# Chained graph layers on one core: orders of their own for the first and last seven turns, VectorE's constants placed later, no filler matmuls

## The chip, the cores and the metric

One core of a Trainium2 chip runs the whole program. The metric is the device time of one execution in microseconds (us); lower is better. TensorE (PE) does the matmuls, VectorE (DVE), ScalarE (ACT) and GpSimd (POOL) the elementwise work, SyncE's queue (SP) starts most of the DMAs. Each engine runs its own list of instructions in order, and they meet only at semaphores.

## What is computed

`x` is (128, 128, 256) and `adj` (128, 128, 128): 128 graphs of 128 nodes. Four layers follow one another, each with its own weights:

```python
def reference(x, adj, ...):
    x = _L0_gnn_ref(x, adj, ...)   # 8-head attention, + log(clip(adj)), out projection, layer norm
    x = _L1_gnn_ref(x, adj, ...)   # one-head attention, logits = q + k^T, mask, leaky relu, softmax
    x = _L2_gnn_ref(x, adj, ...)   # 8-head attention, + a + c^T + log(adj + eps)
    x = _L3_gnn_ref(x, adj, ...)   # like layer 1, other weights
    return x
# layer 0
q = (x @ Wq.T + bq).reshape(b, n, H, DK).transpose(0, 2, 1, 3)      # k, v likewise
logits = jnp.einsum('bhqd,bhkd->bhqk', q, k) / np.sqrt(DK)
logits = logits + jnp.log(jnp.clip(adj, ADJ_MIN, None))[:, None, :, :]
attn = jax.nn.softmax(logits, axis=-1)
out = jnp.einsum('bhqk,bhkd->bhqd', attn, v)
out = out.transpose(0, 2, 1, 3).reshape(b, n, d) @ Wo.T + bo
return _layer_norm(x + out, gamma, beta)
# layer 1
logits = q + jnp.swapaxes(k, 2, 1)
masked = logits + (1.0 - adj_mat) * NEG_INF
masked = jnp.where(masked >= 0, masked, LEAKY_SLOPE * masked)
out = jnp.einsum('bnm,bmh->bnh', jax.nn.softmax(masked, axis=-1), feat_proj)
return out + feats
```

## The kernel before

Two graphs make a group, so there are 64 groups (0 to 63), and every group passes through the four layers. The work of one group is cut into named steps. A step is a name, a layer or stream, and a part; a text that says "`q` of layer 2, group 63" means all instructions of that step. Stream A is the attention of layer 0, stream B that of layer 2.

The steps of an attention layer are, in the order in which they depend on one another:

- `turn_x`: ACT rounds the layer's transposed input to a high part (`xt_hi`), POOL (layer 0) or DVE (the others) makes the low part (`xt_lo`). In layer 1 PE first transposes the input.
- `v`, `k`, `q`: PE multiplies by the weights in three passes of high and low parts (lines 911 to 913, 12 matmuls of 256 columns a step; layer 2's `v` is two parts of 6), ACT moves the result to SBUF.
- `scores`: PE, L976, and in stream B also L985. `max`: DVE takes the least of each row from the four score banks (L800). `max_parts`: two small DVE steps in stream B. `turn_max`: PE turns those (L1079), ACT copies. `again`: the scores turned (L976). `shift`: the maxima are subtracted (L999).
- `soft`: ACT takes the exponentials (L563, L567). `weigh`: DVE multiplies three of four banks by the adjacency (L824), POOL the first (L486).
- `den`: PE sums (L1020), DVE takes the reciprocal and splits it (L831 to L835), POOL spreads it to `inv_parts` (L492). `use`: PE multiplies the weights by `v` (L1011), ACT copies the result. `wide`: PE spreads the reciprocals (L1025), DVE multiplies (L841).
- Layer 0 then has `split` (ACT and DVE halve the result into `ot_hi`, `ot_lo`), `out_proj` in two parts (PE, DVE adds and takes statistics), `rstd` (POOL, L498 and L502) and `norm` (DVE L877, ACT L573). Layer 2 has `sum` (DVE, L848).

Layers 1 and 3 have `fc` in two parts (12 matmuls in all), `mask` (PE L1113, DVE L759), `leak` (ACT, DVE), `exp`, `inv` (ACT, DVE), `turn_p` (PE L1119, ACT copies to `fpt`) and `mix` (PE L1125, DVE adds). `adj_t` and `penalty` prepare the adjacency. SP loads four arrays for each group, each load behind the last reader of the same buffer of the group before.

The table ORDER gives every engine one fixed list of steps for a turn, each step with a lag. Turn t does, in that list's order, step (lag, name) of group t minus lag. So a steady turn holds every step once, of up to seven different groups. In the first and the last turns the steps of groups that do not exist are left out, and what remains keeps its order:

```python
    def steps(self, engine):
        for lag, name, where, n in ORDER[engine]:
            if self.holds(self.t, lag):
```

Eight PSUM banks are shared out by position in TensorE's list. Before a step fills a bank, PE waits until the last reader of the bank's former contents is done (`wait_drained`).

Setup is woven into group 0. DVE first makes small constants (`pick`, `own`, `spread`, `minus_pick`, `low_row`; L684 to L696), then the low parts of the weights (`low_parts(FIRST)`: q0, k0, v0; `low_parts(SECOND)`: five more). Eight steps of groups 0 and 1 on PE are preceded by filler matmuls (L1063), whose result is overwritten:

```python
FILLERS = {(("den", "A", 0), 0): 6, (("out_proj", "0", 0), 0): 12, (("turn_max", "A", 0), 1): 10,
           (("den", "A", 0), 1): 4, (("mix", "1", 0), 0): 5, (("out_proj", "0", 0), 1): 4,
           (("turn_max", "A", 0), 2): 7, (("mix", "1", 0), 1): 5}
```

## Time and profile before

| | |
|---|---|
| median of 3 runs | 1814.74 us (1814.38 to 1816.23) |
| the profiled execution | 1811.3 us, of which the span is 1809.5 us |
| PE busy | 1750.8 us, 97% of the span |
| DVE, ACT, POOL busy | 1474.9, 1371.8, 731.3 us |
| filler matmuls | 53 records, 8.95 us busy |

The span runs from the first to the last instruction. An engine's busy time is the union of its instructions. Matmul ends are modelled, so the distance from start to start is the better measure of a row of matmuls. "Idle before" in a row is the time in which the engine did nothing ahead of that instruction, and the name behind the arrow is what ended it.

### The profile page before, as it was taken

The page shows a single profiled execution, that of the slowest core. Times are in us where ns is not written, and L with a number is a line of the kernel's source. Part 1 is how long each engine was busy: PE and PEld are TensorE (multiplying, and loading weights), DVE is VectorE, ACT ScalarE, POOL GpSimd, SP SyncE. Part 2 cuts the span into 40 slices and gives each one's busy share as a digit, 9 for nine tenths or more (in the row PEclk, how much of TensorE's full clock was granted, in tenths as well). Part 3 has the DMA queues.
Part 4 walks back from the last instruction along what each step waited for, and adds up shares of the span by engine and source line. Part 5 has one row for each costly group of instructions (what it writes and reads, how often), then busy time and mean ns, then how long its engine had stood idle before and what let it go on. Part 6 is the DMA issues. An engine that isn't in the chain of part 4 may idle for free.

```text
span 1809.5 us, 68658 instructions
## 1 busy us (share of the span) xinstructions
PE 1750.8 (97%) x28065; PEld 1642.0 (91%) x28065; DVE 1474.9 (82%) x3361; ACT 1371.8 (76%) x3792; POOL 731.3 (40%) x797
## 2 busy tenths in 40 slices
PE   6899999999999999999999999999999999999985
PEld 6799999999999999999999999999999999999974
DVE  4678888888888888888888888888888888888873
ACT  3577787787787787787877778778778777778773
POOL 3344443443444344344344344444444344344321
PEclk8999999999999999999999999999999999999997
DMA  3011111011011011011011011111111101101100
GB/s 108 28 37 37 37 49 48 26 49 49 26 49 49 26 49 48 26 49 49 27 47 49 30 44 49 38 37 49 34 40 49 49 26 49 47 28 49 35 13 18
DMA packets 48260, 74.55 MB, mean 41 GB/s; under 512 B 5456, under 2 KB 21968, under 8 KB 47952
## 3 DMA queue, kind: packets, MB, share of 16 engines
q1 hardware_dynamic: 47376, 69.49, 12.0%
q8 instruction: 227, 3.72, 0.9%
q10 hardware_dynamic: 576, 0.68, 0.2%
q14 instruction: 81, 0.66, 0.1%
HBM read 53.37 MB, written 16.78 MB: 39 GB/s over the span
## 4 chain that ended last, share of the span: by engine, by line
PE 88%; ACT 3%; DMA 2%; DVE 2%; issue 2%; POOL 2%; SPq 0%; POOLq 0%; DVEq 0%; ACTq 0%
PE banks L911 16%; PE banks L976 14%; PE banks L913 14%; PE banks L912 14%; PE banks L1125 7%; PE banks L1020 6%; PE banks L1011 6%; PE banks L999 3%; DMA x_t<-x_t_dram 2%; PE banks L1025 2%; PE banks L1085 2%; PE banks L1119 2%; PE banks L1113 2%; POOL weights_B L486 1%; PE banks L985 1%
## 5 line engine op out<-in xcount | busy, mean ns | idle before, releaser
L486 POOL TENSOR_TENSOR weights_B<-weights_B,adj 128x512 f32<-128x512 f32 x64 | 115.2, 1801 | 297.4 <-ACT weights_B L567 297.4
L492 POOL TENSOR_TENSOR inv_parts_A<-inv_both_A,own 128x512 fp32r<-128x512 f32 x64 | 66.6, 1041 | 305.0 <-DVE inv_both_A L835 305.0
L800 DVE TENSOR_REDUCE least_cols_A<-banks 128x4 f32<-128x512 f32 x256 | 159.0, 684 | 32.4 <-PE banks L976 32.3
L800 DVE TENSOR_REDUCE least_B<-banks 128x4 f32<-128x512 f32 x256 | 173.2, 681 | 13.6 <-PE banks L985 13.6
L911 PE MATMUL banks<-w_hi_v,xt_hi 128*128 128x258 f32 (+1 forms) x512 | 157.4, 308 | 13.2 <-DVE w_lo_v L677 11.5
L911 PE MATMUL banks<-w_hi_f,xt_hi 128*128 128x258 f32 x512 | 163.5, 319 | 3.0 <-DVE xt_lo L677 1.5
L641 ACT ACTIVATE fp<-banks 128x258 f32<-128x258 f32 x256 | 92.1, 390 | 93.8 <-PE banks L913 93.8
L567 ACT ACTIVATE banks<-banks,v_B 128x256 f32<-128x256 f32 x384 | 153.7, 475 | 0.0
L911 PE MATMUL banks<-xt_hi,w_hi_k 128*128 128x256 f32 x512 | 151.7, 296 | 0.0
L913 PE MATMUL banks<-w_lo_f,xt_hi 128*128 128x258 f32 x512 | 146.3, 286 | 0.0
L1125 PE MATMUL banks<-fpt,fp 128*128 128x128 f32 x1024 | 143.5, 283 | 2.8 <-ACT fpt L662 2.7
L913 PE MATMUL banks<-w_lo_v,xt_hi 128*128 128x258 f32 (+1 forms) x512 | 145.2, 284 | 0.0
L912 PE MATMUL banks<-w_hi_v,xt_lo 128*128 128x258 f32 (+1 forms) x512 | 145.0, 283 | 0.0
L912 PE MATMUL banks<-xt_hi,w_lo_k 128*128 128x256 f32 x512 | 144.9, 283 | 0.0
L912 PE MATMUL banks<-w_hi_f,xt_lo 128*128 128x258 f32 x512 | 144.7, 283 | 0.0
L1125 PEld LDWEIGHTS banks<-fpt,fp 128*128 128x128 f32 x1024 | 130.0, 193 | 16.0 <-issue 15.4
L913 PE MATMUL banks<-xt_lo,w_hi_k 128*128 128x256 f32 x512 | 144.4, 282 | 0.0
L913 PE MATMUL banks<-xt_lo,w_hi_q 128*128 128x256 f32 x512 | 144.0, 281 | 0.0
L912 PE MATMUL banks<-xt_hi,w_lo_q 128*128 128x256 f32 x512 | 143.6, 280 | 0.0
L911 PE MATMUL banks<-xt_hi,w_hi_q 128*128 128x256 f32 x512 | 143.5, 280 | 0.0
L831 DVE RECIPROCAL banks<-banks 128x128 f32<-128x128 f32 x128 | 122.5, 957 | 9.7 <-PE banks L1020 9.7
L458 POOL TENSOR_TENSOR xb_t<-sum_t,out_col 128x512 f32<-128x512 f32 x64 | 66.5, 1039 | 156.2 <-DVE sum_t L848 156.2
(192 smaller groups left out, 6210.4 us busy)
## 6 DMA issues: line engine op xcount, KB each, us to landing
x_t<-x_t_dram SPq DMA_DIRECT2D x64, 256.0 KB, 3.6
x_in<-x_dram SPq DMA_DIRECT2D x64, 256.0 KB, 3.6
out_dram<-x_out SPq DMA_DIRECT2D x64, 256.0 KB, 2.4
adj_t<-adj_t_dram SPq DMA_DIRECT2D x64, 128.0 KB, 3.4
adj<-adj_dram SPq DMA_DIRECT2D x64, 128.0 KB, 2.0
scratch<-weights_dram SPq DMA_DIRECT2D x9, 256.0 KB, 6.9
scratch<-weights_dram ACTq DMA_DIRECT2D x2, 256.0 KB, 4.6
out_bias<-L_gnn_bo_dram ACTq DMA_DIRECT2D x1, 128.0 KB, 6.9
```

The costliest lines, as they stand in the source:

```text
L486: pool.tensor_tensor(units, units, weight_of[where][:, G.four, :, :].unsqueeze(2).broadcast_to([P, GROUP, 2, P]), ALU.mult).then_inc(first ...
L567: last = act.activation(to[:, cols(g, 2 * P)], x[:, cols(g, 2 * P)], ACT.Exp, bias=v["B"][:, G.odd, g, DIM + 1:WIDE], scale=-1.0)
L641: act.activation(fp[where][:, n, :], bank[b][:, 0:WIDE], ACT.Copy).then_inc(fp_ready[where], 1)
L800: dve.tensor_reduce(to, bank[SCORE_BANKS[n]].rearrange("p (u m) -> p u m", u=UNITS), axis=AX.X, op=ALU.min).then_inc(maxed[where], 1)
L831: dve.reciprocal(bank[b][:, 0:P], bank[b][:, 0:P]).then_inc(inverted[where], 1)
L911: pe.matmul(out_ap, left_hi(k), right_hi(k), start=(k == 0), stop=False)
L912: pe.matmul(out_ap, left_lo(k), right_hi(k), start=False, stop=False)
L913: last = pe.matmul(out_ap, left_hi(k), right_lo(k), start=False, stop=(k == KT - 1))
L976: last = pe.matmul(bank[SCORE_BANKS[r]][:, cols(u)], left[row_group(r), G.odd, half, cols(g)], right[row_group(r), G.odd, half, cols(g)], ...
L1011: last = pe.matmul(to[row_group(r), cols(u)], v[s][:, G.odd, g, head:head + HEAD_DIM], weights[s][:, r, cols(u)], start=True, stop=True)
L1020: last = pe.matmul(to[row_group(r), 0:P], sums[:, u, :], weights[s][:, r, cols(u)], start=(u == 0), stop=(u == UNITS - 1), skip_group_chec ...
L1125: last = pe.matmul(to[:, cols(k * GROUP + g)], fp[layer][:, g, cols(k)], fpt[layer][:, g, :], start=True, stop=True)
```

## The change

Three things are changed.

1. Two new tables, EARLY and LATE, give the order of tensor, vector, scalar and gpsimd for their first and last steps (159, 180, 163 and 46 early ones, 86, 86, 110 and 24 late ones). They hold the same steps as before. Between them ORDER applies as it stands. SP's order is not touched. The semaphore counts of the banks are now counted from the resulting list.
2. DVE makes its constants behind `low_parts(FIRST)`.
3. FILLERS is empty.

```diff
+EARLY = {
+    "tensor": [
+        (0, "v", "0", 0), (0, "k", "0", 0), (0, "q", "0", 0), (0, "scores", "A", 0), (0, "turn_max", "A", 0),
...
+LATE = {
+    "tensor": [
+        (-1, "k", "0", 0), (-2, "out_proj", "0", 0), (-1, "q", "0", 0), (-2, "out_proj", "0", 1), (-3, "k", "2", 0),
...
-FILLERS = {(("den", "A", 0), 0): 6, (("out_proj", "0", 0), 0): 12, (("turn_max", "A", 0), 1): 10,
-           (("den", "A", 0), 1): 4, (("mix", "1", 0), 0): 5, (("out_proj", "0", 0), 1): 4,
-           (("turn_max", "A", 0), 2): 7, (("mix", "1", 0), 1): 5}
+FILLERS = {}
...
+def all_steps(engine, groups):
+
+    order = [(t - lag, name, where, n) for t in range(FIRST_LAG, groups + LAST_LAG + 1)
+             for lag, name, where, n in ORDER[engine] if 0 <= t - lag < groups]
+    early = list(EARLY.get(engine, ()))
+    late = [(groups + back, name, where, n) for back, name, where, n in LATE.get(engine, ())]
+    assert sorted(early) == sorted(order[:len(early)]) and sorted(late) == sorted(order[len(order) - len(late):])
+    return early + order[len(early):len(order) - len(late)] + late
...
-            dve.wait_ge(const_ready, CONSTANTS)
-            dve.tensor_reduce(pick[:, :], pick_all[:, :, :], axis=AX.X, op=ALU.add).then_inc(setup_dve, 1)
...
+            def constants():
+                dve.wait_ge(const_ready, CONSTANTS)
+                dve.tensor_reduce(pick[:, :], pick_all[:, :, :], axis=AX.X, op=ALU.add).then_inc(setup_dve, 1)
...
                 if (name, where, n) == ("max", "A", 0):
                     low_parts(FIRST)
+                    constants()
                     low_parts(SECOND)
```

Below, the line numbers of the changed kernel are some 190 higher, since the two tables stand above: its L877 is L684 of the kernel before, its L1105 is L911.

VectorE at the very start, before (the constants are L684 to L696, the low parts L677):

```order
3 L684 TENSOR_REDUCE pick<-pick_all 128x4
4 L685 TENSOR_REDUCE own<-own_all 128x4
5 L688 TENSOR_REDUCE weights_B<-weights_B 128x128
6 L691 CAST spread<-weights_B 128x128
7 L693 TENSOR_TENSOR minus_pick<-pick,minus 128x512
8 L696 TENSOR_REDUCE low_row<-low_all 128x1
9 L817 TENSOR_SCALAR adj<-adj_t 128x256
10 L677 TENSOR_TENSOR w_lo_q<-scratch,w_hi_q 128x2x256
11 L677 TENSOR_TENSOR w_lo_k<-scratch,w_hi_k 128x2x256
12 L677 TENSOR_TENSOR w_lo_v<-scratch,w_hi_v 128x2x256
```

and in the changed kernel:

```order
3 L1011 TENSOR_SCALAR adj<-adj_t 128x256
4 L869 TENSOR_TENSOR w_lo_q<-scratch,w_hi_q 128x2x256
5 L869 TENSOR_TENSOR w_lo_k<-scratch,w_hi_k 128x2x256
6 L869 TENSOR_TENSOR w_lo_v<-scratch,w_hi_v 128x2x256
7 L877 TENSOR_REDUCE pick<-pick_all 128x4
8 L878 TENSOR_REDUCE own<-own_all 128x4
9 L881 TENSOR_REDUCE weights_B<-weights_B 128x128
```

Six constants moved behind the three low parts.

TensorE around `den` of group 0, before (L953 is a setup product, L1063 the fillers, then `den`, `use`, `wide`, and `k` of group 1):

```order
57 L953 MATMUL banks<-cols_tile 128x2 x4
58 L1063 MATMUL banks<-w_hi_q 128x256 x6
59 L1020 MATMUL banks<-weights_A,sums 32x128 x16
60 L1011 MATMUL banks<-weights_A,v_A 32x128 x16
61 L1025 MATMUL banks<-inv_parts_A,spread 128x512
62 L911 MATMUL banks<-xt_hi,w_hi_k 128x256
```

and in the changed kernel:

```order
57 L1147 MATMUL banks<-cols_tile 128x2 x4
58 L1214 MATMUL banks<-weights_A,sums 32x128 x16
59 L1205 MATMUL banks<-weights_A,v_A 32x128 x16
60 L1219 MATMUL banks<-inv_parts_A,spread 128x512
61 L1105 MATMUL banks<-xt_hi,w_hi_k 128x256
```

The six fillers are gone and nothing else moved; the twelve ahead of `out_proj` of group 0 are gone in the same way.

TensorE late in the last turns, before: the last matmul of layer 2's `v` of group 63, `wide` of group 62, then `q` of group 63:

```order
8343 L913 MATMUL banks<-w_lo_v,xt_hi 128x258
8344 L1025 MATMUL banks<-inv_parts_B,spread 128x512
8345 L911 MATMUL banks<-xt_hi,w_hi_q 128x256
8346 L912 MATMUL banks<-xt_hi,w_lo_q 128x256
8347 L913 MATMUL banks<-xt_lo,w_hi_q 128x256
```

and in the changed kernel, from the end of the same `q`:

```order
8346 L1106 MATMUL banks<-xt_hi,w_lo_q 128x256
8347 L1107 MATMUL banks<-xt_lo,w_hi_q 128x256
8348 L1324 MATMUL banks<-ident,c_cols 128x128
8349 L1219 MATMUL banks<-inv_parts_B,spread 128x512
8350 L1170 MATMUL banks<-kt_B,qt_B 128x128 x16
```

`wide` of group 62 moved behind `q` and `turn_rows` (L1324) of group 63, just ahead of that group's `scores`.

TensorE at the last group, before (`shift`, `use`, `den`, `wide` of 63, `turn_p` and `mix` of 62, `fc` of 63):

```order
8377 L999 MATMUL banks<-least_rows_B,minus_pick 128x128 x16
8378 L1011 MATMUL banks<-weights_B,v_B 32x128 x16
8379 L1020 MATMUL banks<-weights_B,sums 32x128 x16
8380 L1025 MATMUL banks<-inv_parts_B,spread 128x512
8381 L1119 MATMUL banks<-ident,logits 128x128 x2
8382 L1125 MATMUL banks<-fpt,fp 128x128 x4
8383 L911 MATMUL banks<-w_hi_f,xt_hi 128x258
```

and in the changed kernel:

```order
8369 L1193 MATMUL banks<-least_rows_B,minus_pick 128x128 x16
8370 L1214 MATMUL banks<-weights_B,sums 32x128 x16
8371 L1205 MATMUL banks<-weights_B,v_B 32x128 x16
8372 L1219 MATMUL banks<-inv_parts_B,spread 128x512
8373 L1313 MATMUL banks<-ident,logits 128x128 x2
8374 L1319 MATMUL banks<-fpt,fp 128x128 x4
```

`den` moved ahead of `use`.

## Rows read from the trace of the kernel before

**Rows 1.** The page: busy time by engine, share of the span, instructions

```profile
PE 1750.8 (97%) x28065; PEld 1642.0 (91%) x28065; DVE 1474.9 (82%) x3361; ACT 1371.8 (76%) x3792; POOL 731.3 (40%) x797
```

**Rows 2.** Stretches: busy PE, PEld, DVE, ACT, POOL, then clock, DMA share, GB/s

```profile
0.00:130.00 130.00, 106.20 (x1439) 98.46 (x1440) 78.51 (x179) 70.58 (x175) 44.17 (x74) 0.93 0.20 60
130.00:1720.00 1590.00, 1582.75 (x25791) 1489.17 (x25792) 1343.88 (x3071) 1253.92 (x3482) 669.76 (x707) 1.00 0.13 41
1720.00:1809.50 89.50, 61.86 (x838) 54.35 (x836) 52.53 (x114) 47.27 (x136) 17.33 (x17) 0.84 0.04 16
```

**Rows 3.** PE's waits in 0 to 130 us: total, times, longest

```profile
PE banks L911 <- DVE w_lo_v L677: 11.5, 1, 11.5
PE banks L1025 <- POOL inv_parts_A L492: 3.8, 3, 2.3
```

**Rows 4.** DVE in order of time, 5 to 88 us: start, duration, line

```profile
5.61 0.17 DVE L684 TENSOR_REDUCE pick<-pick_all 128x4 f32<-128x16 f32 x1 [1.47 <-POOL own_all L440]
...
9.28 0.28 DVE L817 TENSOR_SCALAR adj<-adj_t 128x256 f32<-128x256 f32 x1
...
10.69 0.68 DVE L677 TENSOR_TENSOR w_lo_v<-scratch,w_hi_v 128x512 fp32r<-128x512 f32 x1
...
50.16 2.47 DVE L800 TENSOR_REDUCE least_cols_A<-banks 128x4 f32<-128x512 f32 x4
...
66.74 0.69 DVE L786 TENSOR_TENSOR sum_t<-banks,xb_t 128x512 f32<-128x512 f32 x1 [0.78 <-PE banks L1125]
...
84.74 0.42 DVE L771 TENSOR_REDUCE f_neg_max<-logits 128x2 f32<-128x256 f32 x1
...
87.22 0.95 DVE L831 RECIPROCAL banks<-banks 128x128 f32<-128x128 f32 x1
```

**Rows 5.** ACT in order of time: a weight's high part, and a `norm`

```profile
6.94 0.63 ACT L526 ACTIVATE w_hi_v<-scratch 128x512 fp32r<-128x512 f32 x1 [0.48 <-DMA scratch<-weights_dram]
...
75.36 1.09 ACT L573 ACTIVATE x<-x,less,rstd 128x256 f32<-128x256 f32 x2
```

**Rows 6.** POOL in order of time, at 7 us

```profile
6.90 0.61 POOL L471 TENSOR_TENSOR adj<-adj_t,adj_eps 128x256 f32<-128x256 f32 x1 [1.33 <-DMA adj_t<-adj_t_dram]
```

**Rows 7.** PE in order of time, 12 to 77 us

```profile
12.24 0.41 PE L911 MATMUL banks<-w_hi_v,xt_hi 128*128 128x256 f32 x1
12.46 0.41 PE L912 MATMUL banks<-w_hi_v,xt_lo 128*128 128x256 f32 x1
...
33.63 1.65 PE L1063 MATMUL banks<-w_hi_q 128*128 128x256 f32 x6 [0.72 <-DVE cols_tile L732]
35.22 1.86 PE L1020 MATMUL banks<-weights_A,sums 128*32 128x128 f32 x32
...
43.30 1.78 PE L1063 MATMUL banks<-w_hi_q 128*128 128x256 f32 x12
44.92 0.28 PE L911 MATMUL banks<-w_hi_o,ot_hi 128*128 128x256 f32 x1
...
45.40 0.28 PE L912 MATMUL banks<-w_hi_o,ot_lo 128*128 128x256 f32 x1
...
53.16 0.27 PE L1079 MATMUL banks<-ident,least_cols_A 128*128 128x128 f32 x1
...
76.59 0.63 PE L1085 MATMUL banks<-ident,x 128*128 128x128 f32 x4 [0.60 <-ACT x L573]
```

**Rows 8.** PE in order of time, from 1768 us

```profile
1768.85 0.47 PE L1025 MATMUL banks<-inv_parts_B,spread 128*128 128x512 f32 x1 [2.08 <-POOL inv_parts_B L492]
...
1782.97 1.94 PE L1011 MATMUL banks<-weights_B,v_B 128*32 128x128 f32 x32 [4.03 <-DVE weights_B L824]
1784.64 1.97 PE L1020 MATMUL banks<-weights_B,sums 128*32 128x128 f32 x32
...
1794.69 0.56 PE L911 MATMUL banks<-w_hi_f,xt_hi 128*128 128x258 f32 x1
```

**Rows 9.** DVE in order of time, at 1792 us

```profile
1792.61 0.97 DVE L677 TENSOR_TENSOR xt_lo<-sum_t,xt_hi 128x512 fp32r<-128x512 f32 x1 [0.70 <-ACT xt_hi L596]
```

**Rows 10.** One microsecond of the last turns, columns as in rows 2

```profile
1747.00:1748.00 1.00, 1.00 (x6) 0.95 (x5) 0.00 (x0) 0.58 (x2) 0.00 (x0) 0.50 0.00 0
```

More of the change, by code:

```diff
@@ new lines, with __init__ @@
+class Fills:
+    def __init__(self, groups):
+        self.count, self.before = {}, {}
+        last, counts = {}, [0] * BANKS
+        for g, *key in all_steps("tensor", groups):
+            key = tuple(key)
+            if key not in BANK:
+                continue
+            b = BANK[key]
+            counts[b] += 1
+            self.count[key, g], self.before[key, g] = counts[b], last.get(b, (None, None))
+            last[b] = (key, g)
+    def after(self, G, *key):
+        return self.count[key, G.no]
+    def former(self, G, *key):
+        return self.before[key, G.no]
@@ L321, in product, with steps @@
             return bank[PRODUCT_BANK][:, start:start + width]
-        def run(eng, task, first=FIRST_LAG):
-            for t in range(first, GROUPS + LAST_LAG + 1):
-                task(Turn(t, t % RING, GROUPS, BASE))
+        def steps(engine):
+            for g, name, where, n in all_steps(engine, GROUPS):
+                yield name, where, n, Group(g)
         def last_reader(key, g):
@@ L393, in _ @@
             load_weight("k0")
-            turn(Turn(FIRST_LAG, FIRST_LAG % RING, GROUPS, BASE))
+            first, *others = steps("sync")
+            step(first[0], first[3])
             for n in ("o0", "f1", "k2", "q2", "f1_rows", "f3_rows", "v2", "f3"):
                 load_weight(n)
-            run(sp, turn, FIRST_LAG + 1)
+            for name, _, _, G in others:
+                step(name, G)
             for i in range(2):
@@ L750, in weave_setup, with mask @@
                     score_constants()
-            def mask(layer, G, turn):
+            def mask(layer, G):
                 key = ("mask", layer, 0)
@@ L796, in turn @@
                     if name == "max":
-                        dve.wait_ge(filled[SCORE_BANKS[0]], turn.after(G, "scores", where, 0))
+                        dve.wait_ge(filled[SCORE_BANKS[0]], fills.after(G, "scores", where, 0))
                         to = least["B"][:, n, :] if where == "B" else least_cols["A"][:, n, 0:UNITS]
@@ L894, in turn @@
                     elif name == "mask":
-                        mask(where, G, turn)
+                        mask(where, G)
                     elif name == "leak":
@@ L898, in turn @@
                     elif name == "mix":
-                        residual(where, G, turn)
-            run(dve, turn)
+                        residual(where, G)
+            program()
         @block.tensor
```

213 lines of the change are left out of this document (117 added, 96 removed), and 143 rows, old and new, of tables (EARLY, LATE).

## The prediction

> **What bounds the kernel now.** Read the page's busy times first [rows 1]: PE works 97% of the span, no other engine over 82%. Then the same by stretch [rows 2]. From 130 to 1720 us PE is busy 1582.75 of 1590 us, so that stretch is PE's own work and no order of steps can shorten it by more than 7.3 us. What is left lies at the ends. In the first 130 us PE idles 130 - 106.2 = 23.8 us, in the last 89.5 us it idles 27.6 us, and there the granted clock is below 1 (0.93 and 0.84). The change touches only these ends: EARLY and LATE cover about seven turns each, and the list between them is the old one. So I ask, at each place of the ends where PE waits or does fillers, how much sooner the next real matmul can start, and carry that as a shift. A shift at the start is kept to the end, since the middle has almost no idle time that could swallow it. One at the end counts only if it is on the last group's chain.
>
> **The start, term by term.**
>
> *Constants behind the first low parts.* PE's first matmul waits until 11.5 us for the low part of v's weights [rows 3]. DVE finishes that at 10.69 + 0.68 = 11.37 us [rows 4]; it starts the adjacency step and the low parts at 9.28 because the constants are ahead of them. Without these, the latest inputs are the adjacency, which lands by 6.90 (POOL was idle until then) [rows 6], and v's high part at 6.94 + 0.63 = 7.57 [rows 5]. The stretch from 9.28 to 11.37 is 2.1 us; from 6.95 it ends at 9.05. So 11.4 becomes about 9.05: 2.4 us. The constants run from 5.61 to 9.28 now [rows 4], 3.7 us; in the changed kernel they end at about 12.8. The low parts behind them come 1.3 us later than now or not at all later, and none is needed before v, k, q of group 0 are through PE: 36 matmuls at 0.12 to 0.22 us, 4.3 to 7.9 us from 9.05 on. Without that cover it would cost up to the whole 3.7 us.
>
> *Six and twelve fillers.* Six cost 35.22 - 33.63 = 1.59 us and stand straight ahead of `den` of group 0, whose inputs are ready. Twelve cost 44.92 - 43.30 = 1.62 us ahead of `out_proj` [rows 7]. Nothing hides either: 3.2 us.
>
> *Ten fillers before `turn_max` of group 1.* DVE's `max` ends at 50.16 + 2.47 = 52.63 [rows 4], `turn_max` starts at 53.16 [rows 7]: 0.5 us, not the whole of ten fillers. DVE's `adj_t` of group 1 also leaves the way between the two parts of `out_proj`, another 0.2 us. Together 0.7.
>
> *Group 1 up to `out_proj`.* Four fillers ahead of `den`, four ahead of `out_proj`. At full clock a matmul of 256 columns takes (45.40 - 44.92) / 4 = 0.12 us [rows 7], so each four are worth 0.5 us. DVE's `mix` of group 0, 0.6 us, no longer stands ahead of the low part that `out_proj` waits for (it ran at 66.74) [rows 4]. `k` of group 2 moves into the time in which PE waited for `wide`, where the longest of three waits was 2.3 us [rows 3]. Sum 1.6 to 1.9, I take 1.8.
>
> *Group 2's `turn_max`.* Seven fillers are 0.8 us, and PE waits 0.60 us for `norm` ahead of them [rows 7]. In the new order ACT does this `norm` (75.36) [rows 5] ahead of `v` and the next group's input, and PE does `scores` earlier. Both go: 1.4 us.
>
> *Group 2's `den`.* DVE could take the reciprocal at 84.74 + 0.42 = 85.2 but takes it at 87.22 [rows 4], because `den` on PE and two `max` steps on DVE stand ahead. The new order puts `den` ahead of `scores` B on both. I take 1.7 of the 2.0 us, and count the five fillers behind it in this.
>
> Sum of the start: 2.4 + 3.2 + 0.7 + 1.8 + 1.4 + 1.7 = 11.2 us. As a check, all that could go is PE's idle time past its first matmul, 23.8 - 11.5 = 12.3 us, the 2.4 us at the start, and 53 fillers at 0.12 or more, 6 to 8 us: some 22 us. The sum takes half of it.
>
> **What the clock may take back.** Matmuls of 256 columns start every 0.22 us at the lower level of 1.2 GHz (12.24 to 12.46) and every 0.12 at 2.4 GHz [rows 7]. The clock came back around the twelve fillers, and the 24 matmuls of `out_proj` and `q` behind them ran fast. Without fillers these 24 start earlier, and the trace doesn't show at which level. All fast costs 0, all slow 24 x 0.1 = 2.4 us. I take 1.1 us, as if the clock rose about half way, since `k` of group 1 is 12 dense matmuls just ahead of them. The start then gives 10.1.
>
> A row on the same matter: PE ran at 1.2 GHz in the microsecond from 1747 (0.50) [rows 10], in the last turns, where it is idle 31% of the time [rows 2], while the middle, without idle time, shows 1.00 throughout. By the Trainium skill, "TensorE: Matmul & The Clock Gate", Part 1, "the default state is throttled, and activity releases the throttle", which the trace agrees with at both ends. By that rule the removal of the fillers speaks against this change, and all 24 matmuls would be slow: the gain would be 1.3 us less.
>
> **The end, term by term.**
>
> *`q` of group 63 ahead of `wide` of group 62.* PE waits 2.08 us for `wide`'s input at 1768.85, and `q`, which needs nothing of it, stands behind [rows 8]. Now `q` fills that wait, so `scores` of group 63 start up to 2.08 + 0.3 = 2.4 us sooner. What is next: DVE's `max` of 63 has been moved ahead of `turn_x` of 62, and `turn_max` ahead of `mask`, so DVE doesn't give it back. 2.4.
>
> *`den` ahead of `use`, group 63.* Only `den` leads to the reciprocal; `use` took 1784.64 - 1782.97 = 1.67 us ahead of it, at the low clock [rows 8]. Its own result is copied under the reciprocal and POOL's step. 1.7. (0.9 if that stretch is fast.)
>
> *`turn_p` and `mix` of 62 sooner.* The low part for layer 3 is ready at 1792.61 + 0.97 = 1793.58 [rows 9], but `fc` starts at 1794.69 [rows 8], behind `mix`, since ACT did the copy for `mix` after the new input's high part. ACT's order is turned round: 1.1.
>
> *Before that* DVE takes `out_proj` and `turn_x` of group 63 ahead of work of groups 61 and 60. Each move passes one DVE step of 0.6 to 0.7 us. Between 0 and 1.4; I take 0.7, since other waits stand close behind.
>
> Sum of the end: 5.9 us. Together 10.1 + 5.9 = 16.0. The sum is made against the profiled execution (span 1809.5, total 1811.3, 3.4 under the median). Against the median: 1814.7 - 16.0 = **1798.7 us**.
>
> **Rivals.**
>
> *The next wait takes half.* Each term supposes that the second latest input is not close. Where the order of four engines is changed at once, ACT or DVE may be late instead, and the clock may fall once or twice more at the start (one such fall over 15 dense matmuls costs 1.5 us). With half of the reordering terms (1.8 + 1.4 + 1.7 + 5.9 = 10.8, so 5.4 less) and 2 us more of low clock the gain is 8.6: 1806.
>
> *Loads late.* SP's list is unchanged, but group 2's adjacency load waits for POOL's `adj_t` of group 1, which now stands behind `weigh` and `den` of group 0; the POOL step for group 2 waits for that load, and `rstd` of group 0 stands behind it. Before, POOL idled long there. If the load takes 3 us more than I think, `norm` of group 0 is 3 us late and PE with it: 1801.7.
>
> *The clock stays low (slower than before).* If, with the fillers gone, PE's waits between 45 and 100 us keep it at 1.2 GHz, each dense matmul costs 0.1 us more. It decides from 16 us, that is 160 such matmuls or some 19 us of full-speed work. PE is busy 106.2 of the 118.5 us behind its first matmul [rows 2], so in these 55 us it works some 49, 35 fillers of 4 us among it. The worst is 45 us of work taking some 35 more, less about 6 that idle time swallows: 29 - 16 = 13 us slower, 1828. Against it: the last 89.5 us have more idle time than this stretch would have, and their mean clock is still 0.84, so it was high for two thirds of them [rows 2].
>
> *More than the sum.* If the clock doesn't fall at 1747 us and rises sooner at the start, 1.5 us each, and all second waits are absent, another 5 us: 1791.
>
> **How the numbers follow.** The forecast 0.58, half 0.19, loads 0.07, more 0.11, clock low 0.05. Leaving out the clock case and the outer part of the others, the range is 1791.5 to 1806.5. About 0.2% (3.6 us) is what a measurement of this kernel can tell from no change. Faster by more than that: 0.92; within: 0.04; slower: 0.04.
>
> **What would show it.** In the changed kernel's profile the first matmul is at about 9.1 us; `scores` A of group 4 starts some 10 us sooner; the middle's turn is as long as before; `scores` of group 63 follow its `q` with no `wide` wait between; `den` to reciprocal is direct. The prediction is wrong if PE's clock reads 0.50 for much of 40 to 90 us, if PE waits for `norm` of group 0 by over 2 us (at 43 to 47 us), or if the ends show new waits on ACT of over 1 us.

## The result and the profile after

| | before | after |
|---|---|---|
| median | 1814.04 us (1808.79 to 1816.23, 10 executions) | 1799.18 us (1795.28 to 1805.76, 10 executions) |
| the profiled execution | 1811.3 us, span 1809.5 | 1795.47 us, span 1793.7 |

The ratio is 0.9922 with a 95% interval of 0.9906 to 0.9939: 14.9 us faster in the medians, 15.8 us in the spans of the profiled executions. The forecast was 1798.7. The total was right, and two of its steps were not: what the start won is smaller, and partly given back; what the end won is larger. The experiments below show both.

The page of the kernel after, busy time by engine, and the stretches that answer to [rows 1] and [rows 2] (columns as there). The span is now 15.8 us shorter, so the last line reaches past its end:

```profile
PE 1744.9 (97%) x28012; PEld 1634.7 (91%) x28012; DVE 1474.4 (82%) x3361; ACT 1371.6 (76%) x3792; POOL 731.6 (41%) x797
...
0.00:130.00 130.00, 109.27 (x1484) 100.08 (x1485) 83.64 (x191) 77.24 (x192) 48.49 (x78) 0.92 0.20 60
130.00:1720.00 1590.00, 1583.10 (x25835) 1488.85 (x25838) 1346.00 (x3073) 1254.36 (x3484) 668.53 (x705) 1.00 0.13 41
1720.00:1800.00 80.00, 52.57 (x707) 45.73 (x695) 44.72 (x99) 40.03 (x118) 14.55 (x15) 0.85 0.05 18
```

PE's count fell by 53, the fillers; its busy time by 5.9 us. The middle is as dense as before.

DVE in order of time at the start, and PE's first matmul, which answer to [rows 3] and [rows 4]:

```profile
6.79 0.30 DVE L1011 TENSOR_SCALAR adj<-adj_t 128x256 f32<-128x256 f32 x1 [2.64 <-DMA adj_t<-adj_t_dram]
7.00 1.10 DVE L869 TENSOR_TENSOR w_lo_q<-scratch,w_hi_q 128x512 fp32r<-128x512 f32 x1
...
8.62 0.68 DVE L869 TENSOR_TENSOR w_lo_v<-scratch,w_hi_v 128x512 fp32r<-128x512 f32 x1
9.23 0.15 DVE L877 TENSOR_REDUCE pick<-pick_all 128x4 f32<-128x16 f32 x1
...
9.40 0.55 PE L1105 MATMUL banks<-w_hi_v,xt_hi 128*128 128x256 f32 x1 [9.40 <-DVE pick L877]
```

The low part of `v`'s weights ends at 9.30 and PE starts at 9.40 instead of 11.46: 2.06 us. (The releaser named is `pick`, the DVE instruction that ends nearest; what PE waits for is the row above it.)

PE in order of time, the places that answer to [rows 7]:

```profile
31.58 1.94 PE L1214 MATMUL banks<-weights_A,sums 128*32 128x128 f32 x32 [0.72 <-DVE cols_tile L925]
...
39.78 0.50 PE L1105 MATMUL banks<-w_hi_o,ot_hi 128*128 128x256 f32 x1
...
48.08 0.30 PE L1273 MATMUL banks<-ident,least_cols_A 128*128 128x128 f32 x1 [1.08 <-DVE least_cols_A L994]
...
62.15 0.36 PE L1105 MATMUL banks<-w_hi_o,ot_hi 128*128 128x256 f32 x1 [0.40 <-DVE ot_lo L869]
...
70.44 0.30 PE L1273 MATMUL banks<-ident,least_cols_A 128*128 128x128 f32 x1 [0.31 <-DVE least_cols_A L994]
```

`den` of group 0 starts 3.64 us sooner than before, `out_proj` of group 0 5.14, `turn_max` of group 1 5.08, `out_proj` of group 1 6.51, `turn_max` of group 2 7.45.

PE in order of time in the last turns, which answers to [rows 8]:

```profile
1755.51 0.39 PE L1105 MATMUL banks<-xt_hi,w_hi_q 128*128 128x256 f32 x1
...
1757.67 0.49 PE L1219 MATMUL banks<-inv_parts_B,spread 128*128 128x512 f32 x1 [0.37 <-ACT c_rows L858]
1758.40 1.17 PE L1170 MATMUL banks<-kt_B,qt_B 32*128 32x128 f32 x32 [0.23 <-ACT qt_B L813]
...
1765.08 0.67 PE L1193 MATMUL banks<-least_rows_B,minus_pick 4*128 4x128 f32 x16
1769.82 1.94 PE L1214 MATMUL banks<-weights_B,sums 128*32 128x128 f32 x32 [4.07 <-DVE weights_B L1018]
1771.50 1.96 PE L1205 MATMUL banks<-weights_B,v_B 128*32 128x128 f32 x32
1774.76 0.77 PE L1219 MATMUL banks<-inv_parts_B,spread 128*128 128x512 f32 x1 [1.29 <-POOL inv_parts_B L684]
...
1778.93 0.56 PE L1105 MATMUL banks<-w_hi_f,xt_hi 128*128 128x258 f32 x1
```

`q` of group 63 (1755.51) now stands ahead of `wide` of group 62 (1757.67), and the wait of 2.08 us there is 0.37. `den` stands ahead of `use`.

**A ruler for all kernels.** A group's `scores` A are a mark that every turn holds. The table has, for each profiled execution, how much sooner that mark comes than in the kernel before (its marks: 48.88, 73.73, 100.24, 207.32, 287.86 and 1715.97 us, end of the span 1809.5). The last column is the end's shift less that of group 63: what the last 90 us won alone. It is measured against one execution of the old end, and that one was the shortest of four: from `scores` A of group 63 to the end of the span the old order took 93.5 us in the kernel before, 93.7 in e3, 94.8 in e2 and 96.2 in e1, the new order without fillers 86.4 to 86.6 in six. Against the other three, a value of 6.9 here would be 7.1 to 9.6. The labels are those of the experiments below.

| kernel | group 1 | 2 | 3 | 7 | 10 | 63 | end | end alone |
|---|---|---|---|---|---|---|---|---|
| after | 4.67 | 7.16 | 8.51 | 6.62 | 6.62 | 8.88 | 15.8 | 6.9 |
| e12, the same kernel | 4.46 | 4.28 | 5.64 | 3.78 | 3.74 | 2.69 | 9.7 | 7.0 |
| e1 | 2.59 | 4.30 | 5.17 | 5.17 | 5.16 | 6.88 | 4.2 | -2.7 |
| e2 | 1.76 | 1.77 | 0.24 | 0.23 | 0.23 | -2.85 | -4.1 | -1.3 |
| e3 | 5.48 | 3.37 | 4.76 | 2.90 | 2.90 | 2.31 | 2.1 | -0.2 |
| e4 | 1.14 | 1.14 | -0.43 | -0.44 | -0.45 | -2.83 | 4.1 | 6.9 |
| e5 | 5.33 | 3.20 | 2.49 | 2.52 | 2.52 | 3.24 | 10.3 | 7.1 |
| e6 | 4.51 | 6.99 | 8.39 | 8.80 | 8.80 | 8.96 | 15.9 | 6.9 |
| e7 | 4.34 | 6.83 | 8.20 | 6.34 | 6.32 | 7.19 | 14.7 | 7.5 |
| e8 | 5.08 | 6.69 | 8.07 | 6.27 | 6.28 | 8.07 | 15.0 | 6.9 |
| e9 | 5.42 | 4.04 | 5.40 | 3.50 | 3.48 | 4.12 | 9.3 | 5.2 |
| e10 | 5.69 | 3.51 | 4.86 | 2.95 | 2.93 | 1.43 | 4.2 | 2.7 |
| e11 | 4.23 | 5.85 | 7.22 | 7.10 | 7.08 | 6.31 | 16.6 | 10.3 |

And the times. "Clock" is the mean over a kernel's executions of their mean granted clock; the kernels before beside them had 1812.2 to 1814.0 us in the medians and clocks of 0.985 to 0.986. The record of the clock has no entry before its first fall: in the kernel before it reads 1.00 up to 23 us, though matmuls of 256 columns come every 0.22 us up to 16 us, the pace of 1.2 GHz [rows 7]. These means leave that stretch out.

| kernel | median | ratio, 95% | clock |
|---|---|---|---|
| after | 1799.18 | 0.9922, 0.9906 to 0.9939 | 0.9878 |
| e12, the same kernel | 1798.72 | 0.9927, 0.9910 to 0.9945 | 0.9887 |
| e1, no fillers | 1808.26 | 0.9976, 0.9961 to 0.9990 | 0.9850 |
| e2, constants | 1812.49 | 0.9999, 0.9986 to 1.0013 | 0.9851 |
| e3, start only | 1808.19 | 0.9980, 0.9964 to 0.9996 | 0.9845 |
| e4, end only | 1804.99 | 0.9963, 0.9949 to 0.9977 | 0.9887 |
| e5, old order at the start | 1800.10 | 0.9937, 0.9918 to 0.9957 | 0.9870 |
| e6, start's order cut | 1796.10 | 0.9915, 0.9893 to 0.9937 | 0.9880 |
| e7, fillers at the end | 1797.48 | 0.9920, 0.9900 to 0.9940 | 0.9912 |
| e8, fillers in the start's waits | 1795.28 | 0.9908, 0.9888 to 0.9929 | 0.9910 |
| e9, `den` behind `use` | 1802.04, one execution | | 0.986 |
| e10, `wide` ahead of `q` | 1807.11, one execution | | 0.985 |
| e11, cut and fillers | 1793.27 | 0.9881, 0.9861 to 0.9901 | 0.9946 |

### The profile page after: what moved, and what is told of

Read it like the earlier page. It is cut to its first block, busy times and chain, and to the rows that moved or that the text cites. A ratio compares the mean times of both kernels' runs of the same rounds, so it can differ in the third digit from the quotient of the medians.

```text
span 1793.7 us, 68558 instructions
## 1 busy us (share of the span) xinstructions
PE 1744.9 (97%) x28012; PEld 1634.7 (91%) x28012; DVE 1474.4 (82%) x3361; ACT 1371.6 (76%) x3792; POOL 731.6 (41%) x797
## 4 chain that ended last, share of the span: by engine, by line
PE 90%; DVE 3%; ACT 2%; DMA 2%; issue 1%; POOL 1%; SPq 0%; DVEq 0%; POOLq 0%; ACTq 0%
PE banks L1105 16%; PE banks L1170 15%; PE banks L1107 14%; PE banks L1106 14%; PE banks L1319 7%; PE banks L1214 6%; PE banks L1205 6%; PE banks L1193 3%; PE banks L1219 2%; PE banks L1313 2%; PE banks L1279 2%; PE banks L1307 1%; DMA x_t<-x_t_dram 1%; PE banks L1273 1%; PE banks L1179 1%
## 5 line engine op out<-in xcount | busy, mean ns | idle before, releaser
L684 POOL TENSOR_TENSOR inv_parts_A<-inv_both_A,own 128x512 fp32r<-128x512 f32 x64 | 66.7, 1042 | 301.5 <-DVE inv_both_A L1029 301.5
L1105 PE MATMUL banks<-w_hi_v,xt_hi 128*128 128x258 f32 (+1 forms) x512 | 157.4, 307 | 10.3 <-DVE pick L877 9.4
L1105 PE MATMUL banks<-w_hi_f,xt_hi 128*128 128x258 f32 x512 | 162.9, 318 | 1.8
L1105 PE MATMUL banks<-xt_hi,w_hi_k 128*128 128x256 f32 x512 | 151.3, 296 | 2.6 <-DVE xt_lo L869 1.4
L1319 PEld LDWEIGHTS banks<-fpt,fp 128*128 128x128 f32 x1024 | 129.9, 193 | 16.3 <-issue 15.8
L1105 PE MATMUL banks<-xt_hi,w_hi_q 128*128 128x256 f32 x512 | 143.6, 280 | 0.0
L1018 DVE TENSOR_TENSOR weights_A<-banks,adj 128x512 f32<-128x512 f32 x192 | 125.6, 683 | 9.3 <-ACT banks L755 9.3
```

What stands on the lines that cost most here:

```text
L1018: dve.tensor_tensor(weights[where][:, n, :].rearrange(units, g=GROUP, h=2), bank[SCORE_BANKS[n]].rearrange(units, g=GROUP, h=2), weight_of ...
L1105: pe.matmul(out_ap, left_hi(k), right_hi(k), start=(k == 0), stop=False)
L1319: last = pe.matmul(to[:, cols(k * GROUP + g)], fp[layer][:, g, cols(k)], fpt[layer][:, g, :], start=True, stop=True)
```

## Experiments: which part brings what

**e1: no fillers, nothing else.**

```diff
-FILLERS = {(("den", "A", 0), 0): 6, (("out_proj", "0", 0), 0): 12, (("turn_max", "A", 0), 1): 10,
...
+FILLERS = {}
```

> The kernel before, without its 53 fillers and with nothing else changed. Theory 1 (the fillers are pure delay where nothing else is waited for): the six before `den` of group 0 and the twelve before `out_proj` cost 3.2 us, the four and four of group 1 1.0, the ten before `turn_max` of group 1 0.5, the seven of group 2 0 to 0.8, less 1.1 of low clock behind the missing twelve: 3.6 to 4.4 us faster, `scores` A of group 4 sooner by the same, and granted clock back at 1.00 by 45 us. Theory 2 (the fillers hold the clock up, the slower rival): the clock reads 0.50 in parts of 45 to 100 us and the kernel is no faster, or up to 13 us slower. Theory 3 (nearly each filler stands in a wait for another engine, and the wait stays): under 1.5 us faster.

4.2 us faster (by the interval 1.8 to 7.1), and `scores` A of group 3 sooner by 5.17 and of group 10 by 5.16, somewhat more than the 3.6 to 4.4 expected. Theory 1 holds. The clock came back at 43 us and stayed, so theory 2 falls. In its last turns the clock was down at times at which the kernel before had it up, and 2.7 us went there.

**e2: the constants, nothing else.**

```diff
                     low_parts(FIRST)
+                    constants()
                     low_parts(SECOND)
```

> The kernel before, with VectorE's constants behind the first low parts and nothing else changed. Theory 1 (the first matmul's shift is kept): the first matmul starts at 9.4 instead of 11.46 us, and everything behind it, `scores` A of group 4 and the end among it, is 2.1 us sooner. Theory 2 (the shift is lost at the first wait for another engine, since POOL, ACT and the loads do not start sooner): `scores` A of group 4 is under 1 us sooner and the time within 1 us of before.

The first matmul started at 9.41 us, and group 2 was 1.77 us sooner. Then the clock fell from 88 to 93 us, and 1.5 of it went between groups 2 and 3. The median did not move, but the interval (0.9986 to 1.0013) still holds theory 1's 2.1 us (0.9988), so the time doesn't decide. By the mark at group 3 theory 2 is right, by its reason it isn't: no wait for another engine took the shift, the clock did. The mean clock was 0.0013 under that of the kernel before beside it, worth 1.9 us at the 1.45 us for each 0.001 found below (an estimate). Whether the earlier start itself brings such falls is open; e4, whose start is that of the kernel before, shows one at 90 to 94 us too.

**e3: the start alone** (LATE is empty). **e4: the end alone** (EARLY is empty, fillers and constants as before).

```diff
-LATE = {
...
+LATE = {}
```

> The changed kernel with the old order at the end: the start's order, the constants and no fillers. Theory 1 (start and end add up; 8.5 us won by group 3, some 1.9 given back in groups 3 to 7 by the own order itself): `scores` A of group 4 sooner by 8.0, of group 10 by 6.6, the end by 6.6 plus or minus 2 of stray waits in the middle. Rival (the give-back is chance, the same stray waits that the middle shows everywhere): group 10 is sooner by over 7.5 or by another amount than 6.6 in this run. Second rival (part of the end's gain comes from the start's order, since the middle starts in another phase): the end is sooner by over 9 us.

> The kernel before, with only the new order at the end: old order, fillers and constants at the start. Theory 1 (the four end terms, 2.4 for `q` of group 63 ahead of `wide` of 62, 1.7 for `den` ahead of `use`, 1.1 for `turn_p` and `mix` of 62, 0.7 before that, and some 2 more since the clock does not fall at 1747): 6 to 7 us faster, all of it behind 1720 us of the span, and `scores` A of group 4 unmoved. Rival (the end's gain came because the start had shifted it against the loads and stores): under 4 us faster, and the granted clock falls at 1747 to 1750 us again.

e4: the end won 6.9 us in the last 90, the same as in the changed kernel, and 7.4 in the median, a little over the 6 to 7 expected. Theory 1 holds, and the clock did not fall at the place of 1747 us. (Its profiled execution had lost 2.8 us before group 63, so it won 4.1 in all.) e3: 4.2 us in the median, where 6.6 was expected. Its start is instruction for instruction the changed kernel's, and yet it stands at 4.76 for group 3 where that had 8.51. The 1.9 us between groups 3 and 7 went just the same (4.76 to 2.90): this give-back is no chance. What differs is the clock. The stretches of 45 to 55 us, columns as in [rows 2], of e3:

```profile
45.00:50.00 5.00, 3.83 (x49) 3.26 (x53) 2.81 (x5) 2.83 (x6) 3.68 (x4) 0.55 0.02 5
50.00:55.00 5.00, 4.24 (x28) 3.85 (x25) 1.56 (x4) 2.83 (x6) 1.29 (x1) 0.50 0.28 80
```

and of the changed kernel:

```profile
45.00:50.00 5.00, 2.93 (x70) 2.37 (x63) 3.18 (x6) 3.52 (x8) 3.10 (x4) 1.00 0.02 5
50.00:55.00 5.00, 4.24 (x58) 3.77 (x57) 3.07 (x8) 3.06 (x7) 1.86 (x2) 1.00 0.30 80
```

At 1.2 GHz PE gets through 28 records between 50 and 55 us, at 2.4 GHz through 58. Seven profiled executions have this start without fillers. In the four in which the clock first rose at 34.5 to 35.3 us (e3, e9, e10, e12) it fell again at 45 to 48 and was low for 7 to 14 us; in the three in which it rose only at 41 (after, e6, e7) it didn't. Group 3 stands at 4.8 to 5.6 us in the four, at 8.2 to 8.5 in the three. That the moment of the rise is the cause is not shown: e12 had lost the clock once more at 37.9 and got it back at 41.4, as late as the three, and still lost it at 48.

**e12: the changed kernel once more**, since start and end alone sum to less than both.

> The changed kernel itself, once more. The start alone gave 4.2 us and the end alone 7.4, together 11.7, where both in one gave 14.9 in the medians; the granted clocks were 0.9845, 0.9887 and 0.9878 in the means. Theory 1 (the parts add, and the 3 us between are the scatter of the clock's falls, at about 1.6 to 1.8 us for each 0.001 of the mean clock): 11 to 13.5 us under the kernel before, with a mean clock of 0.986 to 0.9875. Theory 2 (start and end support each other): 14.5 us or more again, at a mean clock of 0.9875 to 0.9885.

14.0 us in the medians, between the two theories, with a clock of 0.9887, above both bands. The two sets of the changed kernel agree (0.9922 and 0.9927). e3 and e4 give 0.0020 + 0.0037 = 0.0057 of 1812 us, 10.3 us, with an uncertainty of some 3.8 (2.9 and 2.5 us in squares); the changed kernel 13.2 to 14.1. The gap of 3 to 4 us isn't resolved, and a part of it lies in the mean clocks. Its profiled execution is one of the four above, so the first one, on which the forecast's terms are read below, is from the better half.

**How much of the scatter is the clock?** Every execution is listed with its time and mean clock. Within a set of executions of one kernel the two go together with a correlation of -0.76 over 155 executions, 1.45 us for each 0.001 of the clock.

**e5: the old order at the start, constants and no fillers kept.**

```diff
-EARLY = {
...
+EARLY = {}
```

> The changed kernel with the old order at the start: constants moved, no fillers, the new order at the end only. Theory 1 (the start's own order wins 1.6 us up to group 3 and gives 1.9 back in groups 3 to 7, so it is worth nothing): `scores` A of group 10 sooner by 6.4 to 7.2, as in the changed kernel with 6.6, and the time within 2 us of the changed kernel, 1798 to 1801. Theory 2 (the own order is worth the 4.9 us that its terms of the prediction hold, 1.8 for group 1, 1.4 and 1.7 for group 2): `scores` A of group 10 sooner by under 4 and the time 3 to 5 us longer than the changed kernel's.

0.9 and 1.4 us over the two sets of the changed kernel in the medians; by the ratios 1.8 to 2.7, with an uncertainty of some 4 us. So the start's own order, as it stands, is worth some 1 to 3 us, nearer to theory 1; the 3 to 5 us of theory 2 are less likely, but not excluded. The mark at group 10 (2.52) says nothing here, since the clock fell twice in this execution, at 46 and at 87 us.

**e6: the start's order cut at group 3.**

```diff
-    early = list(EARLY.get(engine, ()))
+    early = list(EARLY.get(engine, ()))[:EARLY_CUT.get(engine)]
+EARLY_CUT = {"tensor": 89, "vector": 93, "scalar": 98, "gpsimd": 35}
```

> The changed kernel with the start's own orders cut where group 3 has its `scores` B of group 1 done (89 steps of TensorE, 93 of VectorE, 98 of ScalarE, 35 of GpSimd kept), the old order from there. Theory 1 (the 1.9 us given back in groups 3 to 7 come from the own orders' later part, where VectorE takes `out_proj` ahead of two `weigh` of B): turns of 26.8 to 26.9 us from group 3 on, `scores` A of group 10 sooner by the same as of group 3, about 1.9 us more than in the changed kernel where the clock does not fall, and the time 1 to 2 us under the changed kernel's, 1797 to 1798. Rival (the give-back is the price of the earlier start, whatever the order is there, since something must bring the engines into the middle's phase): the same 1.9 us are lost again between groups 3 and 7 or just behind.

Groups 3, 4 and 10 stand at 8.39, 8.79 and 8.80: turns of 26.8 us, nothing given back (in e11, which has the same cut, 7.22, 7.62 and 7.08). Theory 1 holds for the place of the loss. Whether the time follows is likely, not shown: the median is 2.6 to 3.1 us under the changed kernel's, but the intervals overlap, and in the profiled executions both stand at 8.9 to 9.0 by group 63.

Between groups 10 and 63 e6 gained 0.2 us where the changed kernel gained 2.3. Over all executions that stretch took 1425.9 to 1431.2 us (1425.9 and 1429.2 in the two of the changed kernel), with the clock at 1.00 throughout and 7 to 10 us of PE idle between 130 and 1720. Most of this idle time has one source: a load of `x_t` lands late, ACT waits for it, `norm` comes late behind it, and PE waits for `norm`. From 130 to 1720 us of the kernel before ACT waits 9.1 us for `x_t`, in nine groups, and PE 5.3 us for `norm`; in the changed kernel it is 5.5 us, in five groups, and 4.0 us. The groups that are hit depend on the kernel: all nine executions without fillers at the start wait for the load of group 11 (e6 lost 1.7 us there, between its groups 10 and 11), and none of the five with fillers there does. So these waits are not wholly chance, though their sum is not tied to any part of the change. What makes the loads late is open.

Where the give-back comes from. The changed kernel at 113 us, DVE, POOL and then PE in order of time:

```profile
112.87 0.28 DVE L1011 TENSOR_SCALAR adj<-adj_t 128x256 f32<-128x256 f32 x1
113.07 1.78 DVE L869 TENSOR_TENSOR xt_lo<-sum_t,xt_hi 128x512 fp32r<-128x512 f32 x1
...
117.50 1.25 DVE L1018 TENSOR_TENSOR weights_B<-banks,adj 128x512 f32<-128x512 f32 x2
...
112.87 1.44 POOL L678 TENSOR_TENSOR weights_B<-weights_B,adj 128x512 f32<-128x512 f32 x1 [4.54 <-ACT weights_B L759]
...
118.90 1.17 PE L1170 MATMUL banks<-kt_A,qt_A 32*128 32x128 f32 x32 [0.82 <-DVE weights_B L1018]
```

and e6, DVE and POOL:

```profile
112.99 0.68 DVE L870 TENSOR_TENSOR xt_lo<-sum_t,xt_hi 128x512 fp32r<-128x512 f32 x1
...
115.06 1.41 DVE L1019 TENSOR_TENSOR weights_B<-banks,adj 128x512 f32<-128x512 f32 x2
...
112.99 1.84 POOL L679 TENSOR_TENSOR weights_B<-weights_B,adj 128x512 f32<-128x512 f32 x1 [4.54 <-ACT weights_B L760]
```

Two things stand in the table EARLY here that the old order doesn't have: `adj_t` of group 4 is ahead of the low part, and both parts of `out_proj` are ahead of the last two `weigh`, where the old order has one. These end at 118.75 instead of 116.47, and `scores` wait 0.82 us for their bank. 0.28 us of `adj_t` let POOL's step begin first, and the low part took 1.78 us instead of 0.68. The cut takes both things away at once; which of them costs how much wasn't tried apart.

## Experiments: the last turns, and the clock

**e9: `den` of 63 behind `use` again. e10: `wide` of 62 ahead of `q` of 63 again.** One execution each.

```diff
-        (-1, "den", "B", 0), (-1, "use", "B", 0),
+        (-1, "use", "B", 0), (-1, "den", "B", 0),
```

```diff
-        (-1, "q", "2", 0), (-1, "turn_rows", "2", 0), (-2, "wide", "B", 0), (-1, "scores", "B", 0),
+        (-2, "wide", "B", 0), (-1, "q", "2", 0), (-1, "turn_rows", "2", 0), (-1, "scores", "B", 0),
```

> The changed kernel with `den` of group 63 behind `use` again, on TensorE alone. To be read in the last turn, by the distance from the end of `shift` of group 63 to VectorE's reciprocal and from there to the end. Theory 1 (only `den` leads to the reciprocal, `use` lies beside it): the reciprocal comes 1.7 to 2.0 us later behind `shift` where the clock reads 0.50 there (1.0 where it reads 1.00), and all that follows by the same. Rival (ScalarE's copy of `use`, which now comes later than the reciprocal, is as late as GpSimd's parts, so the order of the two moves nothing): under 0.5 us.

> The changed kernel with `wide` of group 62 ahead of `q` of group 63 again, on TensorE alone. Theory 1 (the wait for GpSimd's parts of group 62 stands open while `q` could run): TensorE waits about 2 us ahead of `wide`, `scores` of group 63 start 1.7 to 2.4 us later behind `v` of group 63 than in the changed kernel (8.6 us there), and the end moves by the same. Rival (`scores` wait for ScalarE's copy of `q` or of the row of `soul` anyway, and the filled wait is paid there): under 1 us.

PE in order of time, e9:

```profile
1774.67 1.93 PE L1205 MATMUL banks<-weights_B,v_B 128*32 128x128 f32 x32 [4.22 <-DVE weights_B L1018]
1776.35 1.96 PE L1214 MATMUL banks<-weights_B,sums 128*32 128x128 f32 x32
1781.31 0.47 PE L1219 MATMUL banks<-inv_parts_B,spread 128*128 128x512 f32 x1 [3.00 <-POOL inv_parts_B L684]
```

`shift` of 63 starts at 1769.78, so `wide` comes 11.53 us behind it; in the changed kernel it is 9.68. From `shift` to the end of the span it is 30.42 and 28.62. So the swap is worth 1.8 us, as theory 1 says. e10:

```profile
1764.29 0.47 PE L1219 MATMUL banks<-inv_parts_B,spread 128*128 128x512 f32 x1 [1.21 <-POOL inv_parts_B L684]
...
1767.78 1.17 PE L1170 MATMUL banks<-kt_B,qt_B 32*128 32x128 f32 x32 [1.10 <-ACT qt_B L813]
```

`scores` of 63 come 10.59 us behind `v` (1757.19) instead of 8.62: 1.97 us. Theory 1 holds here too, though PE waits only 1.21 us ahead of `wide` where it says 2; another 1.10 us it waits for ACT's copy of `q` (0.23 in the changed kernel). Two more microseconds went up to `shift`, where the clock fell from 1769 on; that is the order's doing or chance, and one execution can't tell.

**e7: fillers in the waits of group 63.**

```diff
-FILLERS = {}
+FILLERS = {(("den", "B", 0), -1): 28, (("wide", "B", 0), -1): 6, (("mask", "3", 0), -1): 4,
+           (("turn_p", "3", 0), -1): 26, (("mix", "3", 0), -1): 3}
```

> The changed kernel with 67 fillers in the waits of group 63's last steps: 28 ahead of `den`, 6 of `wide`, 4 of `mask`, 26 of `turn_p`, 3 of `mix`. Theory 1 (idle waits bring the clock down to 1.2 GHz, and busy waits keep it at 2.4): the clock reads 1.00 from 1750 us to the end, `den` of group 63 takes 0.9 instead of 1.68 us, the twelve matmuls of `fc` 1.6 instead of 2.9, and the end is 2.5 to 3 us sooner; mean granted clock up by 0.004. Rival (the clock falls there for another reason, or the fillers reach over the end of the waits): no gain, or up to 2 us slower, since fillers at 0.22 us each need 6.2 us ahead of `den` where only 4.07 us are free.

The clock's mean is up by 0.0025 to 0.0034, and yet the end won only 0.5 us more in the profile and the median is 1.2 to 1.7 us under the changed kernel's, well within the intervals. PE, e7 first, then e11, which has 14 fillers there:

```profile
1768.30 5.06 PE L1258 MATMUL banks<-w_hi_q 128*128 128x256 f32 x28 [0.90 <-DVE logits L963]
1773.29 1.08 PE L1215 MATMUL banks<-weights_B,sums 128*32 128x128 f32 x32
...
1769.15 1.92 PE L1261 MATMUL banks<-w_hi_q 128*128 128x256 f32 x14 [0.91 <-DVE logits L966]
1772.27 1.08 PE L1218 MATMUL banks<-weights_B,sums 128*32 128x128 f32 x32 [1.19 <-DVE weights_B L1022]
```

`den` takes 0.90 us from start to start now, as theory 1 says, but the fillers themselves ran into a fall of the clock (0.50 from 1768.5 to 1771.6) and took 4.99 us. Their bank came free only 0.90 us behind `shift`, so they reached 1.8 us past the wait, as the rival says. 14 of them end 1.2 us before `den` may start.

**e8: fillers in the waits of groups 0 to 2, e11: the cut, these fillers, and 49 at the end.**

```diff
+FILLERS = {(("wide", "A", 0), 0): 5, (("turn_x", "1", 0), 0): 6, (("turn_max", "A", 0), 1): 7,
+           (("mask", "1", 0), 0): 5, (("k", "0", 0), 2): 9, (("mix", "1", 0), 0): 3, (("out_proj", "0", 0), 1): 2}
```

In e11 the end has 14 ahead of `den`, 6 of `wide`, 3 of `mask`, 24 of `turn_p` and 2 of `mix`.

> The changed kernel with 37 fillers put into waits of groups 0 to 2, each run of them no longer than the wait it stands in: 5 ahead of `wide` of group 0, 6 of `turn_x`, 7 of `turn_max` of group 1, 5 of `mask`, 9 of `k` of group 2, 3 of `mix`, 2 of `out_proj` of group 1. Theory 1 (a filler in a wait costs nothing and spares a fall of the clock between 45 and 60 us, which one execution showed and another did not): the mean granted clock is up by 0.001 to 0.002, the median 1 to 3 us under the changed kernel's and the scatter smaller. Rival (the falls come whatever stands in these waits): the clock's mean is unchanged and the time equal, or 1 to 2 us longer where fillers run at the low clock and reach over the wait's end.

> The changed kernel with the start's own orders cut at group 3, the 37 fillers in the waits of groups 0 to 2, and 49 in the waits of group 63, only 14 of them ahead of `den` instead of 28 (28 lasted 4.99 us and held `den` up by 1.8; ending the wait in time they would be 14 x 0.12 to 14 x 0.22, 1.7 to 3.1 us). Theory 1 (the three add up, since they lie in different stretches): 2.2 us of give-back gone, 1 to 3 of clock at the start, 1.5 to 2.5 at the end: a median of 1792 to 1795 us, mean granted clock 0.992 to 0.994, `den` of group 63 not held up. Rival (what is won at the start is lost to stray waits of the middle, as 1.6 us of the cut's were between groups 10 and 11, and the clock falls elsewhere): 1795.3 or more, no better than the fillers at the start alone.

e8, columns as in [rows 2]:

```profile
36.00:40.00 4.00, 2.75 (x20) 2.53 (x21) 1.39 (x2) 1.74 (x4) 1.99 (x4) 1.00 0.10 33
...
45.00:50.00 5.00, 4.77 (x71) 4.20 (x72) 3.08 (x5) 3.77 (x9) 3.51 (x4) 1.00 0.02 5
50.00:55.00 5.00, 4.82 (x68) 4.17 (x71) 3.50 (x9) 2.59 (x7) 1.48 (x2) 1.00 0.23 81
```

Here the clock had risen at 36 us and did not fall again, with PE busy 4.77 of 5 us where e3 had 3.83. (That the busy waits held it is argued: the changed kernel was busy only 2.93 of these 5 us and kept the clock too.) Theory 1: median 3.4 to 3.9 us under the changed kernel's, clock up by 0.0023 to 0.0032, scatter 2.0 us (standard deviation) against 2.7 to 3.8. The intervals of the two overlap, so it is likely, not shown.

Theory 1's other half, that these fillers cost nothing, is wrong. e11 has them and e6 has not; both have the cut, and the clock rises at 41 us in both and stays up. At group 3 e6 stands at 8.39 and e11 at 7.22: 1.17 us lost. PE, e6 first, then e11:

```profile
36.78 0.76 PE L1220 MATMUL banks<-inv_parts_A,spread 128*128 128x512 f32 x1 [1.44 <-POOL inv_parts_A L685]
...
57.76 0.39 PE L1106 MATMUL banks<-xt_hi,w_hi_k 128*128 128x256 f32 x1 [1.25 <-ACT heads_A L774]
...
36.47 1.44 PE L1261 MATMUL banks<-w_hi_q 128*128 128x256 f32 x5 [1.21 <-ACT v_A L823]
37.70 0.63 PE L1223 MATMUL banks<-inv_parts_A,spread 128*128 128x512 f32 x1
...
57.99 1.34 PE L1261 MATMUL banks<-w_hi_q 128*128 128x256 f32 x9 [1.25 <-ACT heads_A L777]
```

The fillers write into the bank of the step that they stand ahead of, so they start only when that bank is free. At `wide` of group 0 that left them 0.23 of the 1.44 us, and they took 1.23. At `k` of group 2 the wait is the wait for the bank: it stays at 1.25 us, and nine fillers, 1.17 us, come behind it.

e11: 1793.27 us, ratio 0.9881 (0.9861 to 0.9901), 20 us under the kernel before and 5 to 6 under the changed one; its clock read 0.50 for only 5 us in the last turns (22 in the changed kernel) and its end alone won 10.3 us. The time is in theory 1's band and the clock a little above it, and all five executions (1789.3 to 1794.7) lie under the 1795.3 of the rival. Since the intervals of e8 and e11 overlap, that the parts add is likely, not shown. By its median this is the fastest version here.

## Why the prediction was right, and where it wasn't

**Bound.** As it said: the middle is PE's own work (1583.10 of 1590 us busy after), and all that was changed lies at the ends.

**Constants.** Forecast 2.4, measured 2.06: the low part of `q`'s weights took 1.10 us instead of 0.68.

**Six and twelve fillers.** 3.2 forecast. `den` moved by 1.58 more than the first matmul, `out_proj` by another 1.50: 3.1.

**Ten fillers and `adj_t`.** 0.7 forecast. Between `scores` A and `turn_max` of group 1 the shift grew by 5.08 - 4.67 = 0.4.

**Group 1 up to `out_proj`, group 2's `turn_max`, group 2's `den`.** 1.8, 1.4, 1.7 forecast; 6.51 - 5.08 = 1.4, 7.45 - 6.51 = 0.9, and 8.51 - 7.45 = 1.1 up to group 3 measured. Each is 0.4 to 0.6 short, 1.5 of 4.9 us together: at each of them a next wait stands behind the one that went (1.08 us for `least_cols_A`, 1.2 us of `k` of group 2 for ACT's `heads_A`, the copy of `use`; 0.40 for `ot_lo`). This is the mechanism of the first rival, which takes half of these terms; it took three tenths.

**The clock at the start.** 1.1 us forecast, in one place. In the profiled execution it took 5.14 - 4.67 = 0.5: the clock rose at 40.8 us, so the first five of the 24 matmuls ran slow, where its sum had about half of them and its upper bound all. But the step is mis-sized as a whole: in four of seven executions the clock falls a second time, and the start stands some 3.2 us lower at group 3. The prediction named "once or twice more", at 1.5 us each, as a part of a rival and not of the sum.

**"A shift at the start is kept to the end."** This step failed. 1.9 us of it are given back in groups 3 to 7 in all six executions with the full table EARLY and no fillers at the start (1.86 to 1.91), and e6 shows that the table's later part does it. The forecast asked at which places the new order helps, and not whether its last three turns are as short as the old order's 26.8 us.

**`q` ahead of `wide`.** Forecast 2.4; 1.95 in the comparison, 1.97 in e10. **`den` ahead of `use`.** Forecast 1.7; 1.66 in the comparison, 1.8 in e9. **`turn_p` and `mix` of 62.** Forecast 1.1; 15.76 - 14.85 = 0.9. **Before that.** Forecast 0.7; `v` of group 63 came 2.8 us further ahead. Part of it is that the clock, which the kernel before had at 0.50 in 1747 to 1750 [rows 10], stayed at 1.00, as the rival with more than the sum had it. Less 0.44 lost at `shift`, the end won 6.9 where 5.9 was forecast, and it did so in all six profiled executions with this end and no fillers in it (6.9 to 7.1). The old end is less steady: against its other three executions the same end would have won 7.1 to 9.6. So 5.9 was too low by 1 us at the least, and e4's 7.4 in the medians says the same.

**The sum.** In the profiled executions 8.5 - 1.9 at the start, 2.3 in the middle, 6.9 at the end: 15.8. The forecast's 10.1 + 5.9 = 16.0 met it because a start 3.5 us too good was made up by 1.0 at the end and 2.3 us in the middle, for which the forecast had no term (1.3 of it is PE's shorter wait for `norm` behind late loads, 4.0 instead of 5.3 us). That the total came out within 0.2 us is luck.

**The other rivals.** The loads were not late where that rival has them: PE waits 0.99 us for `norm` of group 0, where the kernel before waits 1.45. The clock did not stay low: its longest second fall was 14 us, between 45 and 60. Of the signs that the prediction named, `scores` A of group 4 came 8.0 us sooner instead of 10 (5.1 in e12), the first matmul at 9.40 instead of 9.1, and one new wait on ACT of over 1 us is there, that of `k` of group 2.
